# An adapter, a folded linear layer and routed experts on one core: the order of three small steps changed, and the first tile's expert weighing split in four

## The reference

```
h      = x @ W.T + b + 2 * (x @ A[slot]) @ B[slot]        # a LoRA layer; one of 32 adapters per sample, rank 16
base   = h @ base_w.T + base_b
hidden = h @ A2.T                                          # 64 wide
p      = softmax(h @ router_w.T)                           # 16 experts
w      = the 2 largest p, divided by (their sum + 1e-6)
out    = x + base + 0.5 * sum over the 2 experts e of w[e] * (hidden @ B2[e].T)
```

## Time and profile before

| what | value |
|---|---|
| timed runs, lowest, median, highest | 103.42, 103.99, 104.17 us |
| profiled execution, its own time | 102.98 us |
| its span, first to last instruction | 101.2 us |
| TensorE busy | 97.4 us, 96% of the span |
| VectorE, ScalarE, GpSimd busy | 66.5, 41.4, 21.3 us |
| granted TensorE clock | 1.00 |

### The profile page before, as it was taken

The page is one execution under the profiler, slowest core; times in us unless marked ns, Lnnn a source line. Parts: engine busy times, 40 slices in busy tenths (PEclk is TensorE's granted clock), DMA queues, the critical chain, the costliest instruction groups (busy, mean ns, idle before and its releaser), DMA issues.

```text
span 101.2 us, 1808 instructions
## 1 busy us (share of the span) xinstructions
PE 97.4 (96%) x572; PEld 88.1 (87%) x572; DVE 66.5 (66%) x184; ACT 41.4 (41%) x100; POOL 21.3 (21%) x34
## 2 busy tenths in 40 slices
PE   6999999999999999999999999999999999999990
PEld 7799999999999899789988997899787787788980
DVE  5729996999389776949917946676468626648101
ACT  1705445878768626554344127110910603012000
POOL 5100002243999970070430050000000000000000
PEclk9999999999999999999999999999999999999999
DMA  2999459999955083386196091470074091750211
GB/s 42 362 363 378 138 111 313 366 410 424 314 118 97 23 220 66 115 185 196 23 254 219 16 266 37 126 198 3 16 188 141 5 268 60 216 198 0 104 58 52
DMA packets 8155, 16.92 MB, mean 167 GB/s; under 512 B 1539, under 2 KB 3971, under 8 KB 8018
## 3 DMA queue, kind: packets, MB, share of 16 engines
q1 hardware_dynamic: 7474, 16.41, 53.2%
q10 hardware_dynamic: 640, 0.40, 1.3%
q0 software_dynamic: 32, 0.00, 0.0%
HBM read 13.28 MB, written 2.16 MB: 153 GB/s over the span
## 4 chain that ended last, share of the span: by engine, by line
PE 93%; DMA 3%; DVE 0%; ACT 0%; issue 0%
PE pair L804 89%; DMA w_raw_all<-w_cat 3%; PE pair L963 1%; PE pair L943 1%; PE pair L945 1%; DVE xn L798 0%; PE pair L920 0%; ACT w_hi_all L416 0%; PE pair L933 0%; PE pair L922 0%; PE pair L912 0%
## 5 line engine op out<-in xcount | busy, mean ns | idle before, releaser
L804 PE MATMUL pair<-e_hi,w_hi_all 128*128 128x512 f32 (+1 forms) x72 | 27.3, 379 | 0.0
L804 PE MATMUL pair<-e_hi,w_lo_all 128*128 128x512 f32 (+1 forms) x72 | 26.7, 370 | 0.0
L804 PE MATMUL pair<-e_lo,w_hi_all 128*128 128x512 f32 (+1 forms) x72 | 26.6, 370 | 0.0
L742 DVE TENSOR_TENSOR exp_raw_all<-w_raw_all 128x512 f32<-128x512 f32 x16 | 10.3, 687 | 10.7 <-DMA w_raw_all<-spill 10.7
L526 ACT ACTIVATE w_hi_all<-exp_raw_all 128x512 fp32r<-128x512 f32 x16 | 9.7, 629 | 15.8 <-DVE exp_raw_all L742 15.8
L804 PEld LDWEIGHTS pair<-e_hi,w_lo_all 128*128 128x128 f32 x72 | 13.6, 188 | 2.5
L804 PEld LDWEIGHTS pair<-e_hi,w_hi_all 128*128 128x128 f32 x72 | 13.6, 189 | 2.4
L804 PEld LDWEIGHTS pair<-e_lo,w_hi_all 128*128 128x128 f32 x72 | 13.6, 189 | 1.8
L749 DVE TENSOR_TENSOR w_lo_all<-exp_raw_all,w_hi_all 128x512 fp32r<-128x512 f32 x16 | 10.4, 689 | 3.1 <-ACT w_hi_all L526 2.5
L804 PE MATMUL pair<-p_hi,w_hi_all 128*128 128x304 f32 x32 | 9.8, 307 | 0.0
L804 PE MATMUL pair<-p_hi,x_hi 128*128 128x304 f32 x32 | 9.8, 305 | 0.0
(11 more groups left out here) (106 smaller groups left out, 166.9 us busy)
## 6 DMA issues: line engine op xcount, KB each, us to landing
w_raw_all<-spill SPq DMA_DIRECT2D x16, 256.0 KB, 3.9
exp_raw_all<-experts SPq DMA_DIRECT2D x4, 512.0 KB, 8.4
xn<-x_n SPq DMA_DIRECT2D x4, 512.0 KB, 7.4
out<-xn SPq DMA_DIRECT2D x7, 256.0 KB, 3.9
w_raw_all<-w_cat SPq DMA_DIRECT2D x3, 552.0 KB, 7.0
xt_raw<-x_t SPq DMA_DIRECT2D x2, 512.0 KB, 7.0
xt_raw<-x_t SPq DMA_DIRECT2D x1, 1024.0 KB, 12.4
c_stack<-c_hi SPq DMA_DIRECT2D x7, 74.0 KB, 4.4
```

The costliest lines, as they stand in the source:

```text
L742: nc.vector.tensor_tensor(g[:, js, :], weight_rows[:, b, js, :], hidden[:, b, :].unsqueeze(1).to_broadcast([P, GH, P]), ALU.mult).then_inc ...
L804: return nc.tensor.matmul(out_ap, lhs, rhs, start=first, stop=last)
```

## The change

Four orders are altered; all else stays. (1) In the fold, ScalarE casts W's block 1 in two halves, the first of which releases TensorE's first two row groups. (2) On TensorE bias() comes before lora_first_transpose(), and on ScalarE the copy of its high part comes before the copy of the transposed first rows. (3) On VectorE split_experts_lo(2) stands behind route(1). (4) Tile 0's g is weighed, and split into its parts, in four pieces of 256 columns with semaphores of their own, and the experts' product waits piece by piece.

```diff
+            act.wait_ge(in_w[1], 16)
+            for cols, done in ((W_LEFT, wh_next), (W_RIGHT, wh_done)):
+                nc.scalar.activation(w_hi[:, 1, cols], w_raw[:, 1, cols], ACT.Copy).then_inc(done, 1)
+            for k in range(2, KC):
...
+            def g_hi_first():
+                for q in range(4):
+                    js = slice(q * GH // 2, (q + 1) * GH // 2)
+                    if q % 2:
+                        act.wait_ge(g_done, q // 2 + 1)
+                    else:
+                        act.wait_ge(g_piece, q // 2 + 1)
+                    nc.scalar.activation(gt_hi[:, 0, js, :], g[:, js, :],
+                                         ACT.Copy).then_inc(gh_done if q % 2 else gh_piece, 1)
...
             lora_first()
             first_rows()
-            lora_first_t()
             act.wait_ge(pe_bias, 1)
             nc.scalar.activation(bias_hi[F_BIAS:FT, :], w2_cols(ps_b)[F_BIAS:FT, :], ACT.Copy).then_inc(bh_done, 1)
+            lora_first_t()
             split_experts(1)
...
             routing_rows(1)
-            g_hi(0, 0)
-            g_hi(0, 1)
+            g_hi_first()
             lora_hi(4)
...
+            def weigh_first():
+                dve.wait_ge(doubled[0], 16)
+                dve.wait_ge(spread[0], 32)
+
+                dve.wait_ge(el_pool_done, 1)
+                for q in range(4):
+                    js = slice(q * GH // 2, (q + 1) * GH // 2)
+                    nc.vector.tensor_tensor(g[:, js, :], weight_rows[:, 0, js, :],
+                                            hidden[:, 0, :].unsqueeze(1).to_broadcast([P, GH // 2, P]),
+                                            ALU.mult).then_inc(g_done if q % 2 else g_piece, 1)
+                    if q:
+                        g_lo_first(q - 1)
+                g_lo_first(3)
+
+            def g_lo_first(q):
+                js = slice(q * GH // 2, (q + 1) * GH // 2)
+                if q % 2:
+                    dve.wait_ge(gh_done, q // 2 + 1)
+                else:
+                    dve.wait_ge(gh_piece, q // 2 + 1)
+                nc.vector.tensor_tensor(gt_lo[:, 0, js, :], g[:, js, :], gt_hi[:, 0, js, :].bitcast(F32),
+                                        ALU.subtract).then_inc(gl_done if q % 2 else gl_piece, 1)
...
             route(0)
-            split_experts_lo(2)
             lora_lo(2)
             read_z(1)
             route(1)
+            split_experts_lo(2)
             lora_lo(3)
             read_z(2)
             route(2)
-            weigh(0, 0)
-            weigh(0, 1)
-            g_lo(0, 0)
-            g_lo(0, 1)
+            weigh_first()
             lora_lo(4)
...
             for k in range(1, KC - 1):
-                pe.wait_ge(wh_done, k + 1)
                 pe.wait_ge(wh_first, k + 2)
                 for m in range(KC):
+                    if k == 1 and m == 0:
+                        pe.wait_ge(wh_next, 1)
+                    elif m == (KC // 2 if k == 1 else 0):
+                        pe.wait_ge(wh_done, k + 1)
                     fold_pass(m, k, w_hi, w_hi, False, False)
...
                 for c in chunks:
-                    if c in (0, GH):
-                        pe.wait_ge(gh_done, 2 * t + (1 if c == 0 else 2))
-                        pe.wait_ge(gl_done, 2 * t + (1 if c == 0 else 2))
+                    if t == 0 and c in (0, GH):
+                        pe.wait_ge(gh_piece, 1 if c == 0 else 2)
+                        pe.wait_ge(gl_piece, 1 if c == 0 else 2)
+                    elif c == (GH // 2 if t == 0 else 0) or c == (GH + GH // 2 if t == 0 else GH):
+                        pe.wait_ge(gh_done, 2 * t + (1 if c < GH else 2))
+                        pe.wait_ge(gl_done, 2 * t + (1 if c < GH else 2))
...
             x_first(0)
             x_other(0)
+            bias()
             lora_first_transpose()
-            bias()
             x_first(1)
```

More of the change, by code:

```diff
@@ L197, in adaln_ffn_kernel @@
         wh_left = sem("wh_left")
+        wh_next = sem("wh_next")
         wh_done = sem("wh_done")
@@ L253, in adaln_ffn_kernel @@
         gl_done = sem("gl_done")
+        g_piece = sem("g_piece")
+        gh_piece = sem("gh_piece")
+        gl_piece = sem("gl_piece")
         pe_d = sem("pe_d")
@@ L423, in _ @@
                 act.dma_start(lora_raw[:, t, :], src).then_inc(in_lora, 16)
-            for k in range(1, KC):
+            act.wait_ge(in_w[1], 16)
+            for cols, done in ((W_LEFT, wh_next), (W_RIGHT, wh_done)):
+                nc.scalar.activation(w_hi[:, 1, cols], w_raw[:, 1, cols], ACT.Copy).then_inc(done, 1)
+            for k in range(2, KC):
                 act.wait_ge(in_w[k], 16)
@@ L734, in weigh @@
                     dve.wait_ge(spread[b], 32 * (t // NB + 1))
[L735 to L741, removed]
+                dve.wait_ge(gh_done, 2 * (t - 1) + half + 1)
+                dve.wait_ge(gl_done, 2 * (t - 1) + half + 1)
                 nc.vector.tensor_tensor(g[:, js, :], weight_rows[:, b, js, :],
```

## The result

Over 22 runs of each kernel the median goes from 103.05 to 103.55 us; the ratio is 1.0054 with a 95% interval of 1.0032 to 1.0077. The change costs 0.56 us (0.3 to 0.8): small, but clear of no change. The ratio is of the fast executions alone, since some of either kernel take about 1% longer, and the medians are of all. The 3 runs shown before the prediction have their median at 103.99; 22 of the same kernel have it 0.9 us lower. The profiled execution took 103.74 us, 0.76 more than the one of before; its span is 101.9 us.

The account below looks back on a forecast made before the run. TensorE bounds the kernel, but its routing transpose would wait for lora_lo(4): 0.06 later start plus 0.59 longer chain is +0.65 us, parts 1 to 3 giving nothing else. From 103.7, taken as 104.4; range 104.1 to 104.6, whole range 103.4 to 105.3.

Parts of the forecast that it names:

- Gaps A to C: TensorE's gaps: A, 0.19 us before L920; B, 0.3 before x_first(3); C, 0.35 from lora_lo(4)'s end to the routing transpose.
- the early first chunk: TensorE's first experts' chunk: ready at 40.68, taken without a wait at 40.95, against 41.36 before.
- a new wait for lora_lo(4): TensorE's routing transpose idles some 1.2 us and runs at 42.91, against 42.26, as lora_lo(4) is queued behind eight pieces.
- W: Start of tile 0's weighing, when the spread weights land: taken as 39.19, 0.06 us later than before.
- the two holes of about 0.23: VectorE's idling in tile 0's weighing: 0.24 us before low part 0 and another 0.24 before low part 3.
- The release: From lora_lo(4)'s end on VectorE to the routing transpose's matmul on TensorE: 0.35 us kept, possibly 0.15.
- ScalarE's queue: Part 2 puts the first rows' copy behind the bias copy: queue 0.18 us later, 0.06 later up to routing_rows(0).
- The tail: The moved VectorE piece, from 34.3, meets only the end of GpSimd's own two pieces, profiled at 29.22 to 34.96.
- the first rival: lora_lo(4) doesn't decide, or tile 0's weights land sooner, W 0.95 us sooner: 0.3 faster, 103.7; chance 0.17.
- The idle wait costing clock: TensorE's idle 1.2 us brings back the slower warm-up matmul pace: about 3 us, 107; chance 0.03.
- No overlap between pieces: VectorE's eight pieces follow every 0.42 us instead of 0.34: +1.3, 105.0; chance 0.06.
- Better overlap and a shorter release: VectorE's pieces overlap better and the transpose is released sooner: +0.1 to +0.4 us, 104.0; chance 0.18.

Follow-up runs that it names:

- a1: The changed kernel with part 4 undone, tile 0 weighed in two halves in the old order; ratio to the kernel before 0.9984.
- a2: The kernel before with part 4 alone, tile 0 weighed in four pieces; ratio to the kernel before 1.0079.
- a3: The changed kernel with lora_hi(4) ahead of ScalarE's four high parts and lora_lo(4) between VectorE's second product and first low part; ratio to the kernel before 0.9920.
- e2: The changed kernel with TensorE's routing_transpose(2) moved behind tile 0's chunks 1 to 3; ratio to the kernel before 0.9930.
- a4: The changed kernel with SyncE's stack_rows(4) moved behind spread_routing(0); ratio to the kernel before 1.0029.

## Why the prediction was right or wrong

**Right: the mechanism and its place.** Gaps A to C, their closing by parts 2 and 3, the early first chunk, and a new wait for lora_lo(4) that eats all of it: each is in the profile after, and a1, a2, a3 and e2 show by their ratios that this wait is the loss.

**Right: the size.** Forecast 0.06 + 0.59 = 0.65 us. Measured 0.56 (0.3 to 0.8) in timed runs and 0.76 in the profiled pair. The chain from W was forecast 0.59 longer and is 0.56; VectorE's spacing of 0.34 is there (40.58, 40.91, 41.24, 41.58), and so are the two holes of about 0.23, before the first low part (0.15 of idling shown behind an end that overlaps) and before the last. The release was 0.36 for 0.35, though it is no constant: in a2 and a4 0.25 us lie between the same two events (42.49 to 42.74 in a2). TensorE's first chunk was forecast at 40.95 and came at 40.88, 0.07 sooner, as block 1 of the fold did (8.65 for 8.72).

**Mis-sized: W.** I had 0.06, from ScalarE's queue alone. That term was itself wrong: the bias copy started 0.07 sooner than forecast (25.87), and the copy of the first rows and split_experts(1) overlap by 0.10, so that queue ran no later (26.73 in both), and the spill was issued 0.19 sooner, not 0.06 later. W came 0.19 later all the same, because the spill took 0.16 longer and the spread 0.22. The prediction called the spread "a steady 3.9 us"; that was a median. From SyncE's issue to the first product it took 4.56 to 5.13 us over these kernels. So this step alone scatters by 0.3 us to either side, half the effect, and the 0.19 of one pair of executions can't be put down to the edit.

**Part 3, the piece on VectorE.** Forecast 1.1 to 2.24 us, measured 1.22, at 34.13, so it ended at 35.35, before the 35.5 to 36.5 forecast. The tail that it was to meet was gone, since GpSimd's pair had ended at 33.99; what met it was a smaller instruction, and GpSimd was the one that waited:

```profile
34.13 1.22 DVE L656 TENSOR_TENSOR e_lo<-exp_raw_all,e_hi 128x1024 fp32r<-128x1024 f32 x1
```

```profile
29.17 4.82 POOL L394 TENSOR_TENSOR e_lo<-exp_raw_all,e_hi 128x1024 fp32r<-128x1024 f32 x2
33.93 0.25 POOL L386 CAST p_hi<-lora_raw 128x64 fp32r<-128x64 f32 x1
34.25 1.28 POOL L388 TENSOR_TENSOR p_lo<-lora_raw,p_hi 128x64 fp32r<-128x64 f32 x1
```

Its pair takes 4.82 (twice 2.41) instead of the 5.74 of the earlier trace rows, and its 64-column subtraction 1.28 instead of the 0.32 to 0.33 that it takes elsewhere: it starts inside VectorE's piece and ends 0.2 after it. Six of the seven other kernels with part 3 show the same (1.27 to 1.31 us); in a4, where VectorE's piece came only at 35.67, the subtraction takes 0.32. The Trainium skill ("SBUF — State Buffer", section "Who interferes with whom") has it that a VectorE instruction with two inputs in SBUF and a GpSimd one that reads SBUF exclude each other, the first to issue holding the shared ports to its end. These traces agree.

**Wrong: what the effect was weighed against, and the base.** Two steps failed, and neither is in the mechanism. The first is in "How the numbers follow": *"Under 1% either way (about 1.04 us) a measurement can't tell from no change."* I put 0.82 on no change with a forecast of 0.6% slower. With 22 runs of each kernel the interval reaches 0.23% to either side, and by that the change is slower, as my own sum said; the chances hid what the sum stated.

The second is the base, at the end of "The sum": *"I forecast from there: 103.7 + 0.65, taken as 104.4."* The 103.7 was the middle of four executions that lie 1.2 us apart (102.98 to 104.17); 22 give 103.05, 0.65 less, which is as much as the whole effect. So the measured 103.55 lies below the forecast's own range (104.1 to 104.6, with a run's spread 103.8 to 104.9), and only the whole range, which goes down to 103.4 for the first rival, takes it in. Of the 0.85 us between 104.4 and 103.55, 0.65 are the base, 0.05 the rounding, and 0.15 the step (0.50 between the medians for 0.65; the ratio makes it 0.56). The rivals weren't on one base either: the first counts from 103.99, the others from 103.7.

**Rivals.** The weights landing sooner: no; the spill never took less than 2.28 us. The idle wait costing clock: no; after 1.69 us without a weight load the 128x512 matmuls follow at 0.233 (3.50/15) and the granted clock reads 1.00. The Trainium skill ("TensorE: Matmul & The Clock Gate", section "What's actually happening") lets idling lower the clock; here 1.69 us without a weight load didn't. No overlap between pieces: no, they follow every 0.34. Better overlap and a shorter release: no in this profile (0.34 and 0.36).

## What to carry to other kernels

Cutting a step into pieces lets its first consumer start sooner and its last instruction end later; look at what is queued behind the last piece, and who waits for that. Here a 0.17 us instruction behind eight pieces held up TensorE; put in a hole between them, or its consumer moved back three chunks, it made the same change a gain: 0.8% and 0.7% over the kernel before. If one engine is the bound, the sum of a change is what happens to its last wait, and savings before that wait count for nothing as long as the wait remains. A forecast of a time needs a base from more than a few runs, however good the forecast of the step. Slack that hangs on a first transfer should be read from more than one execution.

## What the runs showed of the hardware

A wait of over a microsecond in TensorE's stream (1.69 us of idle weight load) left the pace of its matmuls as it was (0.233 us for 512 columns). The landing of a pair of transfers of 256 KB each, issued at the same point of twelve kernels, varied by 0.6 us (4.56 to 5.13 with the issue included); where nothing behind it has slack, as in the changed kernel, that moves the end. And a 64-column subtraction on GpSimd took four times its usual time (1.28 us for 0.32) by coming 0.12 us after a VectorE instruction with two inputs in SBUF.
